# Inputs, lag chunks and weights in another order on one DMA queue, and the engines' work with them

## The chip, the cores and the metric

The kernel runs on one core of a Trainium2 chip. The metric is the device time of one execution in microseconds. An execution with the profiler on gives the trace; all times "at" a point are microseconds from the start of its span.

## The reference

```python
# x, ctx: (32, 128, 256) float32; w, u: (256,)
# 1. bidirectional RWKV mixing over the 128 tokens of a sequence, v = k = ctx, r = layernorm(x)
ek  = exp(k);  cur = exp(u + k)
wkv = (Af + Ab + cur * v) / (Bf + Bb + cur)      # Af[t] = sum over i<t of exp((t-1-i) w + k[i]) v[i], Ab the same from behind
x   = x + tanh(g_xattn) * sigmoid(r) * wkv       # Bf, Bb: the same sums without v
# 2. gated feed-forward in 8-bit steps, width 704
xq  = fake_quant(layernorm(x), clip_x)           # one scale over the whole tensor
h   = fake_quant(silu(xq @ Wgate.T) * (xq @ Wup.T), clip_down)
x   = x + tanh(g_ffn) * (h @ Wdown.T)            # weights quantised by row
```

## The kernel before

The program is written out engine by engine; each engine runs its own list in order and waits on semaphores. It has three stages, and the change lies in the first two.

**Stage 1, inputs (to about 33 us).** The 32 sequences are 8 groups of 4. SP loads x (`load_x`) and the context (`load_ctx`), one 512 KB transfer for a group, all on SP's queue. TensorE reverses each context group in time by a product with a flip matrix (`reverse`, L1043); ScalarE takes its exponential (`exp_k`, L538); VectorE multiplies that by the context (`product`, L742). The reversed groups share three pairs of PSUM banks, so `reverse(g)` waits for `product(g-3)`. For x, VectorE takes mean and variance (`stats1`, L760 and L764), GpSimd the reciprocal root (`rstd1`, L389 to L394) and ScalarE the exponential of the normalised x for the sigmoid (`exp_z`, L546). `idle_products` are products on TensorE whose results nobody reads.

**Stage 2, mixing (33 to 99 us).** The sums over tokens are products with a Toeplitz matrix for each of the 256 channels, 8 channels to a chunk, 32 chunks. ScalarE writes the 255 lag weights of each channel to DRAM once (`lag_weights`, stored with L534), and SP loads each chunk's matrices from there (`load_lags`, L309, 512 KB) into a ring of six slots that the context groups use first. Three chunks (`MADE`) are not loaded: ScalarE makes the exponentials (`make_lags`, L652, 8 instructions), and GpSimd prepares (`own_weights`, L419) and adds (`add_own`, L429) the diagonal. TensorE works the chunks in order (`accumulate(j)`, L1059, 16 matmul records each). The first waits for all eight `product`s; chunk j waits for its matrices and, from j = 6, for `mix(j-6)`, since six PSUM banks hold the sums. Chunks go on in pairs m: VectorE `denominator` (L799), ScalarE `reciprocal` (logarithm L554, exponential L557), VectorE `mix` (L811), GpSimd `residual` (L436). `denominator(0)` also waits for all eight `exp_z`. From pair 10 on, VectorE takes six early statistics for stage 3 in each pair (`early_stats`, L768).

Between the chunks the feed-forward weights are prepared: `load_weights` on SP, row maxima on VectorE (`weight_scales`, L750 to L752; for the third matrix also `down_diagonals`, L839), rounding and casting on ScalarE (`quantise_weights` L591, `cast_weights` L599), 12 transposes on TensorE (`turn_weights`, L1071) and a copy by ScalarE (`keep_weights`, L606, L609). A pair is finished by its last `mix`; the last one of all, `mix(31)`, opens stage 3.

**Stage 3, feed-forward (from 99 us)** begins with statistics of the mixed x. The change doesn't touch it.

A slot of the ring is asked for like this, on SP:

```python
before = GROUPS + j - SLOTS
if before < GROUPS:
    sp.wait_ge(s["ctx_back"], before + 1)
else:
    sp.wait_ge(s["ab_done"], before - GROUPS + 1)
```

Of the kernel before, what the change touches and what calls it, by code (L numbers as in the profile page):

```python
# [41 lines left out]
def gated_rwkv_ffn(nc, x, ctx_kv, g_xattn, g_ffn, w, u, clip_x, clip_down, w_gate, w_up, w_down, out):  # L42
# [4 lines left out]
    GROUPS = SEQS // GS  # L47
# [11 lines left out]
    CHUNKS = C // CK  # L59
# [2 lines left out]
    LAGS = 2 * T - 1  # L62
    SLOTS = 6

    MADE = 10, 14, 18

    BATCHES = [0], [1], [2, 3], [4, 5], [6, 7]
    BY_POOL = 1, 1, 1, 2, 2, 2, 2, 2
# [6 lines left out]
    with ExitStack() as stack:  # L75
# [40 lines left out]
        def loads_to(n):  # L116

            return len([i for i in range(n % SLOTS, n + 1, SLOTS) if i - GROUPS not in MADE])

# [165 lines left out]
        @block.sync  # L285
        def _(sp):
            def load_values(name, src):

                sp.dma_start(S[name], src.rearrange("(a b) -> a b", a=1).broadcast_to([P, 1])) \
                    .then_inc(s[name + "_in"], 16)  # L290

            def load_ctx(g):
                if g >= SLOTS:
                    sp.wait_ge(s["ctx_back"], g - SLOTS + 1)
                sp.dma_start(ring[g % SLOTS].rearrange("p (b c) -> p b c", c=C),
                             ctx_v[:, g * GS:(g + 1) * GS, :]).then_inc(ring_in[g % SLOTS], 16)

            def load_x(g):
                sp.dma_start(seqs(x_all, g * GS, GS), x_v[:, g * GS:(g + 1) * GS, :]).then_inc(x_in[g], 16)

            def load_lags(j):
# [6 lines that stand above are left out]
                src = bass.AP(lag_dram, j * CK * LAGS, [[1, P], [LAGS, CK], [1, T]])  # L308
                sp.dma_start(lag_tile(j), src).then_inc(ring_in[(GROUPS + j) % SLOTS], 16)  # L309

            def load_weights(m):

                if m < 2:
                    src = (w_gate, w_up)[m]
                    rows = w_nat[m].rearrange("p (k c) -> p k c", c=C)
                    sp.dma_start(rows[:, 0:KI, :],  # L316
                                 src[0:KI * P, :].rearrange("(k p) c -> p k c", p=P)).then_inc(weights_in[m], 16)
                    for half in range(2):
                        sp.dma_start(rows[half * IR:(half + 1) * IR, KI, :],
                                     src[KI * P:I, :]).then_inc(weights_in[m], 16)  # L320
                else:
                    down, src = w_nat[m].rearrange("p (h i) -> p h i", h=CH), w_down.rearrange("(h p) i -> p h i", p=P)
                    sp.wait_ge(s["w_quant"], 1)
                    sp.dma_start(down[:, :, 0:I], src).then_inc(weights_in[m], 16)
                    sp.dma_start(down[:, :, I:KA * P], src[:, :, KI * P:I]).then_inc(weights_in[m], 16)

            with nc.allow_non_contiguous_dma("256 values, once"):
                sp.dma_start(wu[:, 0:CG], w.rearrange("a b (p i) -> p (a b i)", i=CG)).then_inc(s["w_in"], 16)
                sp.dma_start(wu[:, CG:2 * CG], u.rearrange("a b (p i) -> p (a b i)", i=CG)).then_inc(s["u_in"], 16)
            load_values("g_x", g_xattn)  # L330
            for g in range(3):
                load_x(g)
            load_ctx(0)
            for g in range(3, 6):
                load_x(g)
                load_ctx(g - 2)
            load_ctx(4)
            load_ctx(5)
            load_x(6)
            load_ctx(6)  # L340
            load_ctx(7)
            load_x(7)
            sp.dma_start(w_all, w.rearrange("a b c -> (a b) c").broadcast_to([P, C])).then_inc(s["w_all_in"], 16)
            sp.dma_start(u_all, u.rearrange("a b c -> (a b) c").broadcast_to([P, C])).then_inc(s["u_all_in"], 16)
            sp.wait_ge(s["lag_stored"], 16)
            for j in range(CHUNKS):
                if j not in MADE:
                    load_lags(j)
                if j == 5:
                    load_weights(0)  # L350
                if j == 9:
                    load_weights(1)
                if j == 16:
                    load_weights(2)
                if j == 20:
                    load_values("g_f", g_ffn)
                    load_values("clx", clip_x)
                    load_values("cld", clip_down)

            for i, n in enumerate(pool_sums):  # L360
                sp.wait_ge(s["sum_done"], i + 1)
                sp.dma_start(out_v[:, 2 * n:2 * n + 2, :], seqs(x_all, 2 * n, 2)).then_inc(s["out_done"], 16)
            sp.wait_ge(s["out_done"], 16 * SUMS)
# [154 lines left out]
        def _(act):  # L518
# [17 lines left out]
            def exp_k(g):  # L536
                act.wait_ge(s["ctx_back"], g + 1)
                nc.scalar.activation(group(ek, g), turned(g).rearrange("p (b c) -> p c b", c=C), ACT.Exp).then_inc(s["ek_done"], 1)  # L538

            def exp_z(g):  # L540

                act.wait_ge(s["sc1_done"], g + 1)
                xs = seqs(x_all[:, :], g * GS, GS)
                for i in range(GS):
                    n = g * GS + i
                    last = nc.scalar.activation(ez[:, n, :], xs[:, i, :], ACT.Exp,  # L546
                                                scale=nr1[:, n:n + 1], bias=mr1[:, n:n + 1])
                last.then_inc(s["ez_done"], 1)
# [37 lines left out]
            def quantise_weights(m):  # L586

                act.wait_ge(s["w_rec"], m + 1)
                cols, parts, inverse = (C, KA, w_inv[:, m, :]) if m < 2 else (KA * P, CH, down_inv)
                for i in range(parts):  # L590
                    last = nc.scalar.activation(w_int[:, i * cols:(i + 1) * cols], w_nat[m][:, i * cols:(i + 1) * cols],  # L591
                                                ACT.Copy, scale=inverse[:, i:i + 1])
                last.then_inc(s["w_quant"], 1)
# [33 lines left out]

            lag_weights()
            for g in range(4):
                exp_z(g)  # L630
                exp_k(g)
            exp_k(4)
            exp_z(4)
            for g in range(5, GROUPS):
                exp_k(g)
            for g in range(5, GROUPS):
                exp_z(g)
            act.wait_ge(s["lag_abs_set"], 1)
            nc.scalar.activation(lag_abs, lag_abs, ACT.Abs).then_inc(s["lag_abs_set"], 1)
# [16 lines left out]
            for m in range(PAIRS - 1):  # L656
                reciprocal(m)
                if 2 * m + 6 in MADE:
                    make_lags(MADE.index(2 * m + 6))
                if m in (3, 7, 11):  # L660
                    quantise_weights((3, 7, 11).index(m))
                if m in (9, 13):
                    keep_weights((9, 13).index(m))
                if m in (5, 9, 13):
                    cast_weights((5, 9, 13).index(m))
                if m == 9:
                    exp_clips()
            for j in (CHUNKS - 2, CHUNKS - 1):
# [61 lines left out]
        def _(dve):  # L730
# [108 lines left out]
                    link(nc.vector.tensor_scalar(down_diag[:, h, :], ident[:, :], down_scale[:, h:h + 1], None,  # L839
                                                 ALU.mult))  # L840

            for g in range(4):
                stats1(g)
            product(0)
            stats1(4)
            product(1)
            stats1(5)
            for g in range(2, 5):
                product(g)
            stats1(6)  # L850
            for g in range(5, GROUPS):
                product(g)
            stats1(7)
            dve.wait_ge(s["lag_abs_set"], 2)
            nc.vector.tensor_scalar(lag_abs, lag_abs, -1.0, 0.0, ALU.add, ALU.max).then_inc(s["lag_abs_done"], 1)
# [3 lines left out]
            for m in range(PAIRS - 2):  # L859
                denominator(2 * m + 2)  # L860
                mix(2 * m)
                denominator(2 * m + 3)
                mix(2 * m + 1)
                if m == 2:
                    weight_scales(0)
                if m == 6:
                    weight_scales(1)
                if m == 9:
                    weight_scales(2)
                    dve.wait_ge(s["ident_set"], 2)  # L870
                    down_diagonals()
                    nc.vector.sem_inc(s["diag_done"], 1)
                if m == 10:
                    sigmoid_clips()
                if m > 9:
                    early_stats(done, 6)
                    done += 6
# [157 lines left out]
        def _(pe):  # L1035
# [58 lines left out]
            idle_products(12)  # L1094
            for g in range(GROUPS):
                reverse(g)
                if g < 4:
                    idle_products(5)
            for j in range(CHUNKS):
                accumulate(j)  # L1100
                if j in (14, 23):
                    turn_weights((14, 23).index(j))
            turn_weights(2)


# [121 lines left out]
```

## Time and profile before

| | us |
|---|---|
| median of 3 executions | 203.07 (202.43 to 203.27) |
| the profiled execution, its own time | 203.11 |
| its span, first to last instruction | 201.4 |
| TensorE busy / VectorE / ScalarE / GpSimd | 176.4 / 157.9 / 148.2 / 123.3 |
| bytes moved by DMA | 30.88 MB |

The profiled execution's own time is 1.7 us above its span, and 0.04 us above the median. Busy time is that of the whole span; on TensorE it contains the idle products.

### The profile page before, as it was taken

Reading aid. Unit: us, or ns where it says so; the run is one execution under the profiler, and the core shown is the slowest. Engines: PE = TensorE matmul, PEld = TensorE weight load, DVE = VectorE, ACT = ScalarE, POOL = GpSimd, SP = SyncE. Lnnn points to the kernel's source line nnn. Section 1 sums busy time; section 2 is a strip of 40 time slices with the busy share of each in tenths; the row PEclk is TensorE's granted clock in tenths of the full one; section 3 lists DMA queues with packets and bytes.
Section 4 is the critical chain, followed back from the end, with each engine's and each line's share of the span. In section 5 each row is a group of like instructions: output and inputs, shape, how many; then the busy total and the mean of one; then the engine's idle time right before and its main releaser. Section 6 shows DMA issues by size and latency. Waiting matters only on the chain.

```text
span 201.4 us, 3400 instructions
## 1 busy us (share of the span) xinstructions
PE 176.4 (88%) x1178; PEld 127.8 (63%) x1178; DVE 157.9 (78%) x355; ACT 148.2 (74%) x214; POOL 123.3 (61%) x142
## 2 busy tenths in 40 slices
PE   4589995997979999999959988999999996869990
PEld 4546643997979999999626753444343432658770
DVE  0669669263855777998999958599999998999992
ACT  3459889657498679559768989999798971999900
POOL 3365302565959935335689960989866772358892
PEclk9969999799999999999996999999999999999997
DMA  3999999999999999992000000000000000035555
GB/s 73 343 359 352 348 343 292 283 293 291 289 281 315 260 227 292 292 292 59 0 2 0 3 0 2 0 0 3 0 0 0 0 3 0 0 104 175 192 172 194
DMA packets 46448, 30.88 MB, mean 153 GB/s; under 512 B 2272, under 2 KB 46176, under 8 KB 46432
## 3 DMA queue, kind: packets, MB, share of 16 engines
q1 hardware_dynamic: 46016, 30.16, 53.0%
q10 hardware_dynamic: 416, 0.52, 0.7%
q8 instruction: 9, 0.15, 0.4%
q14 instruction: 7, 0.06, 0.1%
HBM read 26.22 MB, written 4.46 MB: 152 GB/s over the span
## 4 chain that ended last, share of the span: by engine, by line
PE 34%; DVE 25%; POOL 10%; DMA 10%; issue 6%; SPq 6%; ACT 5%; POOLq 1%; DVEq 0%; ACTq 0%
PE ps L1059 19%; PE ps L1043 8%; DMA hidden<-lag_w 6%; DVE h_peaks L952 6%; DVE z_t L1001 6%; PE ps L1162 4%; DVE hidden L941 4%; DMA hidden<-in_ctx 4%; POOL rs L406 3%; POOL hidden L475 2%; SPq L309 2%; PE ps L1090 2%; DVE z_t L1007 2%; DVE silu_out L1007 2%; SPq L316 2%
## 5 line engine op out<-in xcount | busy, mean ns | idle before, releaser
L1059 PE MATMUL ps<-hidden 128*128 128x128 f32 (+1 forms) x512 | 60.0, 280 | 4.8 <-DVE hidden L742 2.5
L1059 PEld LDWEIGHTS ps<-hidden 128*128 128x128 f32 x512 | 59.3, 196 | 6.0 <-issue 3.3
L436 POOL TENSOR_TENSOR x_all<-x_all,silu_out 128x512 f32<-128x512 f32 x15 | 23.0, 1537 | 19.4 <-DVE silu_out L811 19.4
L799 DVE SCALAR_TENSOR_TENSOR h_space<-z_t,ps 128x256 f32<-128x256 f32 x32 | 19.0, 598 | 12.2 <-PE ps L1059 11.9
L952 DVE TENSOR_REDUCE h_peaks<-hidden 128x1 f32<-128x1024 f32 (+1 forms) x24 | 26.0, 1124 | 0.2
L1198 PE MATMUL ps<-wdT,z_t 128*128 128x256 bf16 x192 | 22.4, 272 | 2.8 <-DVE z_t L1001 2.5
L1198 PEld LDWEIGHTS ps<-wdT,z_t 128*128 128x128 bf16 x192 | 17.8, 97 | 7.6 <-DVE z_t L1001 3.2
L702 ACT ACTIVATE silu_out<-ps,mix_scale 128x1024 f32<-128x1024 f32 (+1 forms) x18 | 18.4, 1020 | 2.1 <-PE ps L1162 2.0
L554 ACT ACTIVATE up_out<-h_space 128x512 f32<-128x512 f32 x15 | 9.4, 627 | 13.5 <-DVE h_space L799 13.5
L546 ACT ACTIVATE z_t<-x_all,mr,nr 128x256 f32<-128x256 f32 x32 | 16.4, 588 | 3.6 <-POOL mr L394 3.6
L1043 PE MATMUL ps<-hidden,flip 128*128 128x512 f32 x32 | 16.2, 647 | 3.2 <-DMA hidden<-in_ctx 3.2
L760 DVE BATCH_NORM_STATS2 bn<-x_all 128x6 f32<-128x256 f32 x32 | 11.2, 413 | 8.4 <-DMA x_all<-in_x 8.2
L811 DVE SCALAR_TENSOR_TENSOR silu_out<-ps,small,silu_out 128x256 f32<-128x256 f32 x32 | 15.2, 477 | 2.7 <-ACT silu_out L557 2.7
L722 ACT ACTIVATE h_space<-hidden,small 128x2560 int16<-128x2560 f32 (+1 forms) x9 | 17.1, 1942 | 0.3 <-DVE z_t L1001 0.3
L499 POOL TENSOR_TENSOR hidden<-h_space 128x1024 f32<-128x1024 f32 x6 | 14.7, 2447 | 3.9 <-ACT h_space L706 3.9
L514 POOL TENSOR_TENSOR x_all<-x_all,z_t 128x512 f32<-128x512 f32 x8 | 10.4, 1295 | 10.4 <-DVE z_t L1007 9.9
L499 POOL TENSOR_TENSOR hidden<-silu_out,up_out 128x1024 f32<-128x1024 f32 x6 | 14.2, 2361 | 3.8 <-ACT up_out L706 3.8
L941 DVE SCALAR_TENSOR_TENSOR hidden<-ps,mix_scale,silu_out 128x1024 f32<-128x1024 f32 (+1 forms) x12 | 13.2, 1101 | 2.9 <-ACT silu_out L702 2.8
L1118 PE MATMUL ps<-wgT,ident_b 128*128 128x512 bf16 x60 | 15.3, 396 | 0.0
L389 POOL TENSOR_TENSOR ve<-mv,consts 128x4 f32<-128x4 f32 x8 | 1.6, 199 | 20.4 <-DVE mv L764 20.4
L768 DVE BATCH_NORM_STATS2 bn<-x_all 128x6 f32<-128x128 f32 x64 | 13.5, 276 | 0.1
L1090 PEld LDWEIGHTS ps<-ident,flip 128*128 128x128 f32 x64 | 10.1, 240 | 5.0 <-POOL ident_b L378 2.8
(117 smaller groups left out, 340.3 us busy)
## 6 DMA issues: line engine op xcount, KB each, us to landing
hidden<-lag_w SPq DMA_DIRECT2D x29, 512.0 KB, 7.6
x_all<-in_x SPq DMA_DIRECT2D x8, 512.0 KB, 8.8
hidden<-in_ctx SPq DMA_DIRECT2D x8, 512.0 KB, 9.1
out<-x_all SPq DMA_DIRECT2D x15, 256.0 KB, 2.1
xq<-in_L_ffn_w_down SPq DMA_DIRECT2D x1, 704.0 KB, 5.8
xq<-in_L_ffn_w_gate SPq DMA_DIRECT2D x1, 640.0 KB, 7.3
h_space<-in_L_ffn_w_up SPq DMA_DIRECT2D x1, 640.0 KB, 6.0
out<-x_all ACTq DMA_DIRECT2D x1, 256.0 KB, 2.7
```

The costliest lines, as they stand in the source:

```text
L436: nc.gpsimd.tensor_tensor(xs, xs, mixed[:, m % 2, :, :].rearrange("p c b -> p b c"), ALU.add).then_inc(s["x1_done"], 1)
L499: nc.gpsimd.tensor_tensor(hidden[:, b * HB + k * BT:b * HB + (k + 1) * BT], silu_even[n % 2], up_even[n % 2], ALU.mult).then_inc(s["h_even ...
L546: last = nc.scalar.activation(ez[:, n, :], xs[:, i, :], ACT.Exp, scale=nr1[:, n:n + 1], bias=mr1[:, n:n + 1])
L702: nc.scalar.activation(silu_out[:, 1, 0:cols] if k % 2 else silu_even[even % 2], banks[0], ACT.Silu, scale=mix_scale[:, 0, k:k + 1]).then_ ...
L722: nc.scalar.activation(dst, inner(b, i, last, k, end), ACT.Copy, scale=S["inv_h"]).then_inc(s["h_int"], 1)
L799: nc.vector.scalar_tensor_tensor(den[:, m % 2, i * HALF:(i + 1) * HALF].rearrange("p (c b) -> p c b", b=SEQS), ez[:, :, j * CK:(j + 1) * C ...
L941: nc.vector.scalar_tensor_tensor(hidden[:, b * HB + k * BT:b * HB + k * BT + cols], ps[:, 6:8, :].rearrange("p a n -> p (a n)")[:, 0:cols] ...
L952: nc.vector.tensor_reduce(h_peaks[:, KA * b + k:KA * b + k + 1], hidden[:, b * HB + k * BT:b * HB + k * BT + cols], AX.X, ALU.max, apply_a ...
L1043: last = nc.tensor.matmul(turned(g)[:, half], flip[:, :], ring[g % SLOTS][:, half], start=True, stop=True)
L1059: last = nc.tensor.matmul(ps[:, j % BANKS, c * 2 * SEQS:end * 2 * SEQS], lag_tile(j)[:, c, :], ekp[:, (j * CK + c) * 2 * SEQS:(j * CK + en ...
L1118: nc.tensor.matmul(ps[:, bank, :], ident_b[:, :], wgT[:, 0, 0:512], start=True, stop=True)
L1198: last = nc.tensor.matmul(ps[:, n % 8, j * C:(j + 1) * C], hq[b % 2][:, at_:at_ + P], wdT[:, tile, :], start=(k == 0 and j == 0), stop=(k ...
```

## The change

It changes only the order of work; every instruction stays, and there are ten more idle products (20 stood between the reversals; now 16 stand between them and 14 behind them).

```diff
-    MADE = 10, 14, 18
+    MADE = 8, 12, 16
...
-            for g in range(3):
-                load_x(g)
+            load_x(0)
             load_ctx(0)
-            for g in range(3, 6):
-                load_x(g)
-                load_ctx(g - 2)
+            load_x(1)
+            load_ctx(1)
+            load_ctx(2)
+            load_x(2)
+            load_ctx(3)
             load_ctx(4)
+            load_x(3)
             load_ctx(5)
+            load_ctx(6)
+            load_x(4)
+            load_ctx(7)
+            load_x(5)
+            sp.wait_ge(s["lag_stored"], 16)
+            load_lags(0)
             load_x(6)
-            load_ctx(6)
-            load_ctx(7)
             load_x(7)
...
-            sp.wait_ge(s["lag_stored"], 16)
-            for j in range(CHUNKS):
+            for j in range(1, CHUNKS):
                 if j not in MADE:
                     load_lags(j)
-                if j == 5:
+                if j == 11:
                     load_weights(0)
-                if j == 9:
+                if j == 15:
                     load_weights(1)
-                if j == 16:
+                if j == 22:
                     load_weights(2)
...
             for g in range(4):
+                if g > 0:
+                    exp_k(2 * g - 1)
+                exp_k(2 * g)
                 exp_z(g)
-                exp_k(g)
-            exp_k(4)
-            exp_z(4)
-            for g in range(5, GROUPS):
-                exp_k(g)
-            for g in range(5, GROUPS):
+            exp_k(GROUPS - 1)
+            for g in range(4, GROUPS):
                 exp_z(g)
...
-                if m in (3, 7, 11):
-                    quantise_weights((3, 7, 11).index(m))
-                if m in (9, 13):
-                    keep_weights((9, 13).index(m))
-                if m in (5, 9, 13):
-                    cast_weights((5, 9, 13).index(m))
+                if m in (6, 8, 12):
+                    quantise_weights((6, 8, 12).index(m))
+                if m in (10, 13):
+                    keep_weights((10, 13).index(m))
+                if m in (7, 11, 14):
+                    cast_weights((7, 11, 14).index(m))
...
-            for g in range(4):
+            stats1(0)
+            stats1(1)
+            for g in range(3):
+                product(g)
+            stats1(2)
+            product(3)
+            product(4)
+            for g in range(3, 6):
                 stats1(g)
-            product(0)
-            stats1(4)
-            product(1)
-            stats1(5)
-            for g in range(2, 5):
-                product(g)
+                product(g + 2)
             stats1(6)
-            for g in range(5, GROUPS):
-                product(g)
             stats1(7)
...
-                if m == 2:
+                if m == 5:
                     weight_scales(0)
-                if m == 6:
+                if m == 7:
                     weight_scales(1)
-                if m == 9:
+                if m == 10:
                     weight_scales(2)
...
-                if g < 4:
-                    idle_products(5)
+                if g % 2 == 0:
+                    idle_products(4)
+            idle_products(14)
             for j in range(CHUNKS):
                 accumulate(j)
-                if j in (14, 23):
-                    turn_weights((14, 23).index(j))
+                if j in (20, 25):
+                    turn_weights((20, 25).index(j))
```

Where the change moves instructions: first SP's queue from the inputs to the weights (L309 is a chunk of lag matrices, L316 and L319 one of the first two weight matrices, L324 and L325 the third).

```order
-L299 DMA x_all<-in_x 128x4x256 x3
-L295 DMA hidden<-in_ctx_1024 128x4x256
...
-L343 DMA xq<-in_L0_xattn_w 128x256
-L344 DMA xq<-in_L0_xattn_u 128x256
-L309 DMA hidden<-lag_w 128x8x128 x6
+L309 DMA hidden<-lag_w 128x8x128
+L299 DMA x_all<-in_x 128x4x256 x2
+L349 DMA xq<-in_L0_xattn_w 128x256
+L350 DMA xq<-in_L0_xattn_u 128x256
+L309 DMA hidden<-lag_w 128x8x128 x10
```

One chunk now stands ahead of the last two groups of x, and ten (in place of six) ahead of the first weight matrix.

Then VectorE around the third weight matrix (L750/L754 row maxima, L839/L843 diagonals, L833/L837 and L834/L838 the clips, L768/L772 early statistics, L799/L803 and L811/L815 denominators and mixes). Before:

```order
L750 TENSOR_REDUCE small<-xq 128x2
L751 TENSOR_SCALAR small<-small 128x2
L752 RECIPROCAL small<-small 128x2
L839 TENSOR_SCALAR down_diag<-ident,small 128x128 x2
L799 SCALAR_TENSOR_TENSOR h_space<-z_t,ps 128x256
L811 SCALAR_TENSOR_TENSOR silu_out<-ps,small,silu_out 128x256
L799 SCALAR_TENSOR_TENSOR h_space<-z_t,ps 128x256
L811 SCALAR_TENSOR_TENSOR silu_out<-ps,small,silu_out 128x256
L833 TENSOR_SCALAR small<-small 128x1
```

And now:

```order
L803 SCALAR_TENSOR_TENSOR h_space<-z_t,ps 128x256
L815 SCALAR_TENSOR_TENSOR silu_out<-ps,small,silu_out 128x256
L754 TENSOR_REDUCE small<-xq 128x2
L755 TENSOR_SCALAR small<-small 128x2
L756 RECIPROCAL small<-small 128x2
L843 TENSOR_SCALAR down_diag<-ident,small 128x128 x2
L837 TENSOR_SCALAR small<-small 128x1
L838 RECIPROCAL small<-small 128x1
L837 TENSOR_SCALAR small<-small 128x1
L838 RECIPROCAL small<-small 128x1
L772 BN_STATS bn<-x_all 128x6 x6
```

The maxima and diagonals stood ahead of pair 10's denominators and mixes (chunks 22, 23) and now stand behind them, in one piece with clips and statistics.

Last, ScalarE at the end of stage 2 (L599/L604 the cast of the third matrix, L565/L570 and L568/L573 the half reciprocals of chunks 30 and 31). Before:

```order
L606 ACTIVATE wuT<-ps 128x1536
L599 ACTIVATE w_intb<-w_int 128x1536
L554 ACTIVATE up_out<-h_space 128x512
L557 ACTIVATE silu_out<-up_out 128x512
L565 ACTIVATE up_out<-h_space 128x256
L568 ACTIVATE silu_out<-up_out 128x256
```

And now:

```order
L611 ACTIVATE wuT<-ps 128x1536
L559 ACTIVATE up_out<-h_space 128x512
L562 ACTIVATE silu_out<-up_out 128x512
L604 ACTIVATE w_intb<-w_int 128x1536
L570 ACTIVATE up_out<-h_space 128x256
L573 ACTIVATE silu_out<-up_out 128x256
```

The cast stood ahead of the last whole reciprocal (pair 14) and now stands between it and the half reciprocal of chunk 30.

## Rows read from the trace of the kernel before

**Rows 1.** The page: granted TensorE clock in 40 slices; group of the reversals

```profile
PEclk9969999799999999999996999999999999999997
...
L1043 PE MATMUL ps<-hidden,flip 128*128 128x512 f32 x32 | 16.2, 647 | 3.2 <-DMA hidden<-in_ctx 3.2
```

**Rows 2.** Chain of waits, 80 to 125 us: start us, us, what

```profile
82.49 10.73 PE ps L1059 x96
...
98.83 0.45 DVE silu_out L811
```

**Rows 3.** Timeline, TensorE, 30 to 100 us: start us, us, engine, line, xcount [idle <-releaser]

```profile
33.47 12.53 PE L1059 MATMUL ps<-hidden 128*128 128x128 f32 x96 [2.46 <-DVE hidden L742]
47.16 9.14 PE L1059 MATMUL ps<-hidden 128*128 128x128 f32 x80 [1.16 <-DMA hidden<-lag_w]
57.45 7.38 PE L1059 MATMUL ps<-hidden 128*128 128x128 f32 x64 [1.14 <-DMA hidden<-lag_w]
...
65.33 16.49 PE L1059 MATMUL ps<-hidden 128*128 128x128 f32 x144
...
82.33 14.46 PE L1059 MATMUL ps<-hidden 128*128 128x128 f32 x128
```

**Rows 4.** Two windows: busy us of each engine, granted clock, DMA share, GB/s

```profile
15.00:30.00 15.00, 15.00 (x63) 8.78 (x62) 11.71 (x35) 13.30 (x23) 4.69 (x13) 1.00 1.10 349
30.60:69.06 38.46, 33.70 (x285) 32.92 (x284) 22.46 (x46) 28.24 (x63) 26.30 (x29) 0.96 1.10 292
```

**Rows 5.** DMA issue of u, the last before the chunks: KB, median us to landing

```profile
xq<-in_L_xattn_u SPq DMA_DIRECT2D x1, 128.0 KB, 6.5
```

**Rows 6.** Timeline, 0 to 45 us, and TensorE's weight loads at 69 us

```profile
13.87 1.41 DVE L760 BATCH_NORM_STATS2 bn<-x_all 128x6 f32<-128x256 f32 x4 [1.76 <-DMA x_all<-in_x]
14.56 1.02 ACT L538 ACTIVATE hidden<-ps 128x1024 f32<-128x1024 f32 x1 [2.37 <-PE ps L1043]
...
24.05 0.43 SPq L344 DMA_DIRECT2D xq<-in_L_xattn_u  x1
...
29.82 3.50 DVE L742 TENSOR_TENSOR hidden<-hidden,ps 128x1024 f32<-128x1024 f32 x3
...
34.67 0.38 DVE L764 BATCH_NORM_AGGREGATE mv<-bn 128x2 f32<-128x6 f32 x4
...
36.88 2.08 ACT L546 ACTIVATE z_t<-x_all,mr,nr 128x256 f32<-128x256 f32 x4 [0.89 <-POOL mr L394]
...
39.32 1.10 DVE L799 SCALAR_TENSOR_TENSOR h_space<-z_t,ps 128x256 f32<-128x256 f32 x2
...
40.54 0.63 ACT L554 ACTIVATE up_out<-h_space 128x512 f32<-128x512 f32 x1 [1.08 <-DVE h_space L799]
...
69.10 7.00 PEld L1059 LDWEIGHTS ps<-hidden 128*128 128x128 f32 x62 [0.17 <-DMA hidden<-lag_w]
```

**Rows 7.** Timeline, 45 to 60 us: the made chunk 10 on ScalarE and GpSimd

```profile
47.85 2.44 ACT L652 ACTIVATE hidden<-down_row,xq 128x128 f32<-128x128 f32 x8
49.20 1.28 POOL L429 TENSOR_TENSOR hidden<-hidden,up_out 128x512 f32<-128x512 f32 x1 [0.57 <-ACT hidden L652]
...
51.85 1.04 POOL L419 TENSOR_TENSOR up_out<-flip,xq 128x512 f32<-128x512 f32 x1
...
53.84 1.55 POOL L436 TENSOR_TENSOR x_all<-x_all,silu_out 128x512 f32<-128x512 f32 x1
```

**Rows 8.** Timeline, 79 to 99 us: VectorE's and ScalarE's end of stage 2

```profile
79.19 1.75 DVE L750 TENSOR_REDUCE small<-xq 128x2 f32<-128x1536 f32 x1
...
82.98 0.58 DVE L799 SCALAR_TENSOR_TENSOR h_space<-z_t,ps 128x256 f32<-128x256 f32 x1
...
85.81 0.58 DVE L799 SCALAR_TENSOR_TENSOR h_space<-z_t,ps 128x256 f32<-128x256 f32 x1
...
92.84 1.48 ACT L599 ACTIVATE w_intb<-w_int 128x1536 bf16<-128x1536 int8 x1
...
98.78 0.48 DVE L811 SCALAR_TENSOR_TENSOR silu_out<-ps,small,silu_out 128x256 f32<-128x256 f32 x1
```

## Prediction

> **What bounds the kernel now.** I read the chain of waits from its end first. From 82.5 us to 93.2 it is TensorE's chunk products, and from there to the last `mix` (it ends at 99.26) it is VectorE [rows 2, 8]. Behind that `mix` come stage 3's statistics and the feed-forward, which this change leaves alone. So the change is worth what it moves the end of `mix(31)`, and the rest of the text works that out.
>
> Next TensorE's timeline [rows 3]. A chunk takes 1.81 us (14.46 / 8, and 9.14 / 5 = 1.83). TensorE starts the chunks at 33.47, 2.46 us after its last reversal, released by the last `product`; it waits 1.16 and 1.14 us for loaded chunks 6 and 11, a last 0.17 at 69.1 for chunk 17 [rows 6], and from then on it is never idle: chunk 23 ends at 81.82 and chunk 31 at 96.8. Before 69 us stage 2 hangs on the queue, behind it on TensorE, at the very end on VectorE.
>
> The windows [rows 4] tell what the queue delivers: 349 GB/s while x and context come (1.50 us for 512 KB), 292 GB/s with chunks and weights (1.80 us a chunk, about TensorE's own pace). The reader is to see that two equal paces leave no room to catch up.
>
> **The inputs.** The fifth transfer landed at 13.87 [rows 6] (it was x group 3; it is context 2 now). From there, by durations: reversal 1.7 to 2.0 us (16.2 / 8, some at half clock [rows 1]), exponential 1.0 and `product` 1.2 (3.50 / 3) [rows 6], so `product(2)` ends near 17.9. Behind it VectorE's list has four `stats1` (1.41 + 0.38 + gaps, 1.9 each) and five `product`s, 13.6 us, and 0.6 of waiting for exponential 5, which stands behind `exp_z(2)`: `product(7)` ends at 32.1 and chunk 0 starts at 32.2, **1.3 us earlier**. TensorE's own list is no bound: context 7 is the thirteenth transfer, landing near 25.3, and with the 14 idle products TensorE is free near 30. That the eight context groups land 3 us earlier is thus half lost to VectorE.
>
> Two `stats1` now follow `product(7)`, not one. The last ends at 35.9, against 35.05 (34.67 + 0.38) [rows 6]; GpSimd's root and `exp_z(7)` follow as before, so `denominator(0)` starts at 40.2, **0.9 us later** than 39.32 [rows 6]. x 7 is in by 31.6, so its own lateness is hidden by VectorE. Chunks 0 to 5 need no `mix`, so this late start alone holds nobody up.
>
> **The made chunks.** Chunk 8's exponentials follow the second reciprocal. From `denominator(0)`: two denominators 1.1, reciprocal 1.3 (twice 0.63 [rows 6]), `mix` and `denominator(3)` 1.2, reciprocal 1.3, small gaps: 45.3. The whole piece on ScalarE and GpSimd took 3.9 us for chunk 10 (47.85 to 51.7, the second sum ending 1.28 + 1.27 behind 49.20 [rows 7]), so chunk 8 is ready at 49.2. TensorE, starting at 32.2, is through chunk 7 at 46.7, or near 47.5 with chunks 0 to 7 at the queue's pace: it waits some **2 us** at chunk 8. Even so chunk 8 starts earlier than before (47.16 + 2 x 1.81 = 50.8). From 8 to 16 GpSimd does, for every made chunk, two `own_weights` instructions, two `residual`s and two sums: 2.1 + 3.1 + 2.5 = 7.7 us [rows 7], where TensorE needs 7.3 for four chunks. Chunks 12 and 16 wait 0.4 us each: chunk 16 at 64.5. Then five chunks, one transposition (0.67, from 81.82 to 82.49 [rows 2, 3]) and two more: by TensorE and GpSimd chunk 23 could start at 78.0.
>
> **The queue.** Between u's landing (24.05 + 6.5 = 30.6 [rows 5, 6]) and chunk 17 (69.1) it delivered 16 chunks and three weight matrices, in 38.5 us. Now chunk 0 goes ahead, u lands near 32.4 (one chunk, 1.8, more in front), and up to chunk 23 come 20 chunks and again all three matrices: 38.5 + 4 x 1.81 = 45.7, so chunk 23 lands at 78.1, and the small values at chunk 20 make it 78.4. The weights are not taken off the path; they only move from ahead of chunk 17 to ahead of chunk 23. The queue and the made chunks give about the same time. I take 78.4 as start and 80.2 as **the end of chunk 23, 1.6 us earlier** than 81.82. Bounds: what a matrix costs the queue can be read three times. From 30.6 to 47.16 it brought 7 chunks and one matrix, 16.5 - 12.7 = 3.9 us; from there to 57.45 4 chunks and one, 3.0; to 69.1 5 chunks and one, 2.6 [rows 3, 6]. With all three at 2.6 chunk 23 lands at 76.7 (then GpSimd's 78.0 holds, and it ends at 79.8); with all at 3.9 at 80.6, and it ends at 82.4.
>
> The Trainium skill ("DMA: Bandwidth & Descriptors", Specifications) gives 512 B as the least transfer for line rate. The lag matrices' pieces are 512 B (128 float32), so by that rule chunks would land at x's pace, 1.50 us; the queue would then never bound chunk 23, and the sum would go by GpSimd's 79.8: 203.0. The trace disagrees: 292 against 349 GB/s [rows 4], and the measurement decides.
>
> **VectorE's end.** Behind the end of chunk 23 VectorE has, in order: `denominator(23)`, `mix(21)`, clips and statistics, as from 82.98 to 85.81, 2.8 us; now also the third matrix's maxima and diagonals, 79.19 to 82.98 less a denominator and a `mix`, 2.9 us; then everything from 85.81 to 99.26, 13.45 us, less about 0.5 that it waited in there for chunk 29 (the chain passes from TensorE to VectorE there [rows 2, 8]). That is 18.7. ScalarE adds to it: the cast (1.48 [rows 8]) now stands between the last whole reciprocal and the half one. Counted from `denominator(29)` the half reciprocal comes after 1.3 + 1.5 + 0.9 = 3.7 us, VectorE asks for it after 3.1: 0.6. Together `mix(31)` ends 19.3 us behind chunk 23, at **99.5**. Before it was 17.4. The maxima stood ahead of chunk 22's denominator then, in part while VectorE would have waited. TensorE's gain of 1.6 is spent on 2.9 of maxima and 0.6 of cast behind it, less the wait gone and less what VectorE had fallen behind.
>
> **Nothing or nearly.** The first two matrices' steps on VectorE and ScalarE sit where six banks give chunks a lead: `mix(11)` at 62 and chunk 17, which needs it, at 66. If that cover were gone each would cost what the third's does, some 2 us on VectorE. The transpositions are two between chunks before and after; the first now lies ahead of chunk 21, not 15, which changes no sum to chunk 23 (one before, one now: the second moved from behind 23 to behind 25). SP's wait for the stored lags is met: ScalarE issues the store ahead of its first exponential, and SP reaches the wait behind 14 transfers. Ten more idle products fill a wait.
>
> **Sum.** -1.6 (chunk 23) +1.9 (the way from there) = +0.3 us on the profiled 203.11, which is 0.04 above the median of the runs: **203.4**.
>
> **Rival A, faster.** TensorE's lead is kept. If the GpSimd pieces overlap better than chunk 10's row (chunk 8 ready by 48) and a matrix costs 2.6 us throughout, chunk 23 ends at 78.6, and `mix(31)` at 97.9: 1.4 us gained, 201.7. For it: the matrices cost less and less down the old queue, so the first one's 3.9 may be of its place. Against it: VectorE's 19.3 us are a row-by-row sum with no slack in it. Chance 0.24.
>
> **Rival B, slower.** The queue becomes the bound of the whole second half. Stage 2's transfers have 1.80 us a chunk against TensorE's 1.81; a matrix placed ahead of chunk 23 has no later stretch in which it is made good. Decisive is chunk 23's landing: each us beyond 78.4 goes through to the end. At 3.9 us a matrix it lands at 80.6, `mix(31)` ends at 101.7, 2.4 later: 205.5. For it: the waits at chunks 6 and 11 came right behind matrices [rows 3]. Against it: the third cost less than the first. A landing later than 79.2 turns the result to slower. Chance of that 0.20.
>
> **Rival C, the clock.** TensorE idles some 2 us ahead of chunk 0 and again ahead of chunk 8. Behind the idle 2.46 us ahead of the old chunk 0 the granted clock was at the 1.2 GHz level for a part of slice 8, which reads 7 [rows 1], and the first six chunks took 12.53 - 6 x 1.81 = 1.7 us too long [rows 3]. In the first place that is covered by the wait at chunk 8 (48.4 against 49.2). In the second it would cost up to 1.7 more: 205.1. It is part of B's chance.
>
> **Chances.** A measurement of this kernel tells about 0.5%, 1.0 us, from no change. Forecast, within that: 0.56; A 0.24; B with C 0.20. The range reaches down to A's price and up to 204.9, just short of C's; what is left out is B's far end and a little below A, under 2 in 10.
>
> **What would show it.** Chunk 0 near 32.2; `denominator(0)` near 40.2; an idle TensorE of about 2 us ahead of chunk 8, released by GpSimd's L434; the maxima L754 of the third matrix starting near 81.2; the last L815 ending near 99.5. Wrong if chunk 23 ends before 79 or after 81.5, or if VectorE needs other than 19 us behind it.

## The result and the profile after

The change makes the kernel slower, by about 1%. Both kernels were timed on the same chip, six runs each, and the change was timed a second time on another chip beside the first of the experiments on it:

| | before, us | the change, us | ratio, 95% interval |
|---|---|---|---|
| first comparison | 203.04 (201.47 to 203.27) | 204.52 (204.13 to 205.5) | 1.0094 [1.0056, 1.0131] |
| second | 202.73 | 204.28 | 1.0112 [1.0073, 1.0151] |
| profiled execution: own time, span | 203.11, 201.4 | 204.78, 203.0 | |
| end of chunk 23 | 81.82 | 81.91 | |
| end of the last `mix` | 99.26 | 100.90 | |
| last `mix` to the end of the span | 102.1 | 102.1 | |

The ratios here and below, but not the medians, leave out single executions more than 1.5% above the fastest of their kernel; there is one each in `e1_inputs_only`, `a1_scales9` and `a3_both`.

203.4 had been forecast, +0.3 us; it came out at +1.5. Behind the last `mix` the two kernels take the same 102.1 us (201.4 - 99.26, 203.0 - 100.90), so the whole loss lies ahead of the last `mix`, in the stages that the change touches, as the prediction had it.

The page of the kernel after: granted clock in 40 slices, and the groups of the reversals and of the chunk products.

```profile
PEclk9999999699999999999999999999999999999998
...
L1047 PE MATMUL ps<-hidden,flip 128*128 128x512 f32 x32 | 15.3, 611 | 1.8 <-DMA hidden<-in_ctx 1.7
...
L1063 PE MATMUL ps<-hidden 128*128 128x128 f32 (+1 forms) x512 | 59.8, 280 | 5.0 <-DMA hidden<-lag_w 3.9
```

Slice 8 of the clock reads 6 (7 before [rows 1]): in this execution too the granted clock fell to the 1.2 GHz level once in stage 2, here from 37.5 to 40.9 us, behind the wait for chunk 1. The reversals wait 1.8 us for context and not 3.2, and what the chunk products still wait for is mostly the queue: 3.9 of their 5.0 us.

TensorE's timeline of the kernel after, 30 to 101 us; a chunk is x16.

```profile
32.19 1.97 PE L1063 MATMUL ps<-hidden 128*128 128x128 f32 x16 [1.09 <-DVE hidden L746]
36.48 37.57 PE L1063 MATMUL ps<-hidden 128*128 128x128 f32 x320 [2.32 <-DMA hidden<-lag_w]
...
74.56 3.74 PE L1063 MATMUL ps<-hidden 128*128 128x128 f32 x32
79.90 5.63 PE L1063 MATMUL ps<-hidden 128*128 128x128 f32 x48 [1.61 <-DMA hidden<-lag_w]
...
86.04 10.88 PE L1063 MATMUL ps<-hidden 128*128 128x128 f32 x96
```

Chunk 0 runs alone, TensorE waits 2.32 us for chunk 1 to land, then twenty chunks follow without a gap (those of [rows 3] had waits at 6, 11 and 17). They take 37.57 us where 20 x 1.81 is 36.2; the difference is the slow stretch of the clock. It shows no cost at the end, since TensorE still waits 1.61 us for chunk 23 to land. That wait comes behind the load of the third matrix; chunk 23 starts at 79.90, as before (79.87). TensorE ends chunk 31 at 96.9, as before (96.8).

VectorE's timeline, 76 to 101 us: L803 is a denominator, L815 a `mix`, L754 the maxima of the third weight matrix.

```profile
78.84 0.47 DVE L815 SCALAR_TENSOR_TENSOR silu_out<-ps,small,silu_out 128x256 f32<-128x256 f32 x1
81.94 0.60 DVE L803 SCALAR_TENSOR_TENSOR h_space<-z_t,ps 128x256 f32<-128x256 f32 x1 [2.63 <-PE ps L1063]
82.45 0.48 DVE L815 SCALAR_TENSOR_TENSOR silu_out<-ps,small,silu_out 128x256 f32<-128x256 f32 x1
82.85 1.75 DVE L754 TENSOR_REDUCE small<-xq 128x2 f32<-128x1536 f32 x1
...
98.50 0.48 DVE L815 SCALAR_TENSOR_TENSOR silu_out<-ps,small,silu_out 128x256 f32<-128x256 f32 x1 [0.46 <-ACT silu_out L573]
...
100.42 0.48 DVE L815 SCALAR_TENSOR_TENSOR silu_out<-ps,small,silu_out 128x256 f32<-128x256 f32 x1
```

This is the view that tells the story. VectorE stands idle for 2.63 us until chunk 23 is through (79.90 + 2.01 = 81.91, the first `x16` of the chain below), and right behind that wait it does the maxima and diagonals, which in [rows 8] stood ahead of the same denominator, from 79.19. From 81.9 on VectorE is the bound.

The chain of waits of the kernel after, 59 to 99 us: start us, us, what.

```profile
59.93 11.50 PE ps L1063 x103
71.43 8.43 DMA hidden<-lag_w
79.90 2.01 PE ps L1063 x16
81.94 0.60 DVE h_space L803
...
82.93 1.67 DVE small L754
...
95.04 0.64 ACT up_out L559
...
96.24 0.14 ACT w_intb L604
...
97.61 0.41 ACT up_out L570
...
98.50 0.48 DVE silu_out L815
```

Before, the chain stayed with TensorE until 93.2 us and crossed to VectorE there [rows 2]. Now a landing hands it to TensorE for one chunk, and it crosses to VectorE at 81.94, at chunk 23. From there it passes through the maxima, and at 96.24 through the cast of the third matrix on ScalarE (L604), which the half reciprocal (L570) stands behind. Both had been priced.

### The profile page after: what moved, and what is told of

It is laid out like the page before. It is cut to its first block, busy times and chain, and to the rows that moved or that the text cites. A ratio compares the mean times of both kernels' runs of the same rounds, so it can differ in the third digit from the quotient of the medians.

```text
span 203.0 us, 3440 instructions
## 1 busy us (share of the span) xinstructions
PE 176.8 (87%) x1198; PEld 128.1 (63%) x1198; DVE 157.7 (78%) x355; ACT 148.6 (73%) x214; POOL 123.2 (61%) x142
## 4 chain that ended last, share of the span: by engine, by line
DVE 29%; PE 29%; DMA 13%; POOL 10%; issue 7%; ACT 6%; SPq 2%; POOLq 1%; DVEq 0%; ACTq 0%
PE ps L1063 18%; DMA hidden<-lag_w 8%; DVE h_peaks L956 6%; DVE z_t L1005 6%; PE ps L1047 5%; DMA hidden<-in_ctx 5%; PE ps L1167 4%; DVE hidden L945 4%; POOL rs L411 3%; DVE bn L772 2%; POOL hidden L480 2%; DVE z_t L1011 2%; DVE h_space L803 2%; DVE silu_out L815 2%; DVE silu_out L1011 2%
## 5 line engine op out<-in xcount | busy, mean ns | idle before, releaser
L803 DVE SCALAR_TENSOR_TENSOR h_space<-z_t,ps 128x256 f32<-128x256 f32 x32 | 19.1, 599 | 11.9 <-PE ps L1063 11.6
L815 DVE SCALAR_TENSOR_TENSOR silu_out<-ps,small,silu_out 128x256 f32<-128x256 f32 x32 | 15.2, 477 | 3.7 <-ACT silu_out L562 2.8
L1047 PE MATMUL ps<-hidden,flip 128*128 128x512 f32 x32 | 15.3, 611 | 1.8 <-DMA hidden<-in_ctx 1.7
L1094 PEld LDWEIGHTS ps<-ident,flip 128*128 128x128 f32 x84 | 12.1, 223 | 5.2 <-POOL ident_b L383 2.8
L1094 PE MATMUL ps<-ident,flip 128*128 128x128 f32 x84 | 12.3, 307 | 2.8 <-POOL flip L386 2.8
L1123 PE MATMUL ps<-wgT,ident_b 128*128 128x512 bf16 x60 | 14.4, 379 | 0.0
```

The source lines that it names most:

```text
L803: nc.vector.scalar_tensor_tensor(den[:, m % 2, i * HALF:(i + 1) * HALF].rearrange("p (c b) -> p c b", b=SEQS), ez[:, :, j * CK:(j + 1) * C ...
L815: nc.vector.scalar_tensor_tensor(mixed[:, m % 2, i * CK:(i + 1) * CK, :], half_bank(j, 1), S["tanh_x"], rden[:, m % 2, i * HALF:(i + 1) * ...
L1047: last = nc.tensor.matmul(turned(g)[:, half], flip[:, :], ring[g % SLOTS][:, half], start=True, stop=True)
L1094: nc.tensor.matmul(ps[:, TURN, 0:P], flip[:, :], ident[:, :], start=True, stop=True)
```

## The experiments

Two measures are used throughout: the median against the kernel before on the same chip, and, in the profiled execution, the way from the end of chunk 23 to the end of the last `mix` (17.4 us before, 19.0 in the change). The end of a chunk is the end of its sixteenth product. Five executions with the change's queue ended chunk 23 anywhere between 80.4 and 82.1 us, so a verdict rests on medians, and on the way behind chunk 23, which repeats to 0.2 us where VectorE's list is the same.

### One part of the change at a time

`e1_inputs_only`: the new order of inputs, exponentials, products and early statistics, all else as before. It was timed twice, the second time as `e1b_inputs_only`; the trace of the first has a span of 457.9 us and tells nothing, so the rows are the second's.

```diff
-    MADE = 8, 12, 16
+    MADE = 10, 14, 18
...
-                if j == 11:
+                if j == 5:
                     load_weights(0)
```

(and so on for every weight step, back to its place in the kernel before).

> Only the order of the inputs (SP, ScalarE, VectorE, idle products, chunk 0 ahead of x 6 and 7); made chunks and weights as before. Two parts theory (the loss is the third matrix ahead of chunk 23 plus its maxima and cast behind it): no loss worth the name here, 202.5 to 203.5 us, TensorE starts chunk 0 near 32.2, and the last mix ends within 0.5 us of 99.3. Rival, the inputs (the queue loses 2 us around chunk 0 and x 6, as u landed at 34.65 and not 32.4): the whole 1.5 us are here, 204.5 us, last mix near 100.9, chunk 17 landing 70.5 or later.

> The order of the inputs alone once more, since the profile of the first run is unusable: 203.3 us, 0.3 per cent above before. In the profile chunk 0 starts near 32.2 and denominator(0) 0.7 to 1.0 us later than 39.3; the queue is through with chunk 17 no earlier than 69.1.

Measured: 203.34, ratio 1.0034 [1.0016, 1.0051], and again 203.09, 1.0012 [0.9992, 1.0032]. The 1.5 us are not here, and the earlier start buys nothing. TensorE's timeline of the second:

```profile
32.08 1.97 PE L1063 MATMUL ps<-hidden 128*128 128x128 f32 x16 [0.93 <-DVE hidden L746]
35.96 9.16 PE L1063 MATMUL ps<-hidden 128*128 128x128 f32 x80 [1.91 <-DMA hidden<-lag_w]
47.32 18.07 PE L1063 MATMUL ps<-hidden 128*128 128x128 f32 x144 [2.20 <-DMA hidden<-lag_w]
```

What chunk 0 gains is waited out at chunk 1 (1.91) and at chunk 6 (2.20), both times for the queue.

`e2_made_only`: the kernel before with chunks 8, 12 and 16 made on chip.

```diff
-    MADE = 10, 14, 18
+    MADE = 8, 12, 16
```

> Only chunks 8, 12, 16 made in place of 10, 14, 18. Two parts theory: 203.0 plus or minus 0.5; chunk 8 is ready near 48.3, ahead of its turn at 50.8, and the number of loaded chunks ahead of chunk 19 is the same. Rival, GpSimd (7.7 us of work for four chunks that TensorE does in 7.3): a wait for chunks 12 and 16, up to 1 us lost, 204.

Measured: 203.3, 1.0038 [1.0016, 1.0059]. TensorE waits 2.07 us at chunk 6, for a landing, and the chunk 8 behind it costs no wait; GpSimd, the rival, holds nobody up, and the small loss has no cause shown.

`e3_weights_only`: the kernel before with all weight steps moved as in the change, the queue's loads included.

```diff
-                if j == 5:
+                if j == 11:
                     load_weights(0)
...
-                if m in (5, 9, 13):
+                if m in (7, 11, 14):
-                    cast_weights((5, 9, 13).index(m))
+                    cast_weights((7, 11, 14).index(m))
...
-                if m == 9:
+                if m == 10:
                     weight_scales(2)
```

> Only the weights' places (loads behind chunks 11, 15, 22, and their maxima, rounding, casts, copies, transpositions); inputs and made chunks as before. Two parts theory: TensorE is ahead in the middle, then waits at chunk 23 for the queue, which lands near 78 to 79.5; the last mix comes 19.2 us behind chunk 23's end (17.4 before), so 99 to 100.5: 203.0 to 204.3 us. Rival, the inputs: no loss here, 202.5 to 203.0.

Measured: 202.88, 1.0011 [0.9986, 1.0035], no difference. Its profile shows both sides that the prediction weighed: chunk 23 ends at 80.3, 1.5 us earlier than in the kernel before, and the way from there is 19.0 us, 1.6 longer, as in the change; the last `mix` ends at 99.27, where it did. With the old inputs the forecast exchange takes place.

`e4_inputs_made`: the change with the weight steps where they were before.

> The whole change without the weights' part. Two parts theory: all that cost time is out: 202.3 to 203.3 us, last mix 17.5 us behind chunk 23's end. Rival, the inputs: 204.5 us, as the change itself.

Measured: 203.45, 1.0053 [1.0026, 1.008], just above the 202.3 to 203.3 that were expected, though the way behind chunk 23 is 17.4 us, as in the kernel before. Its profiled execution was its fastest (202.6), with the last `mix` ending at 98.65, so the profile alone would have told a gain where the median tells a loss.

The parts give 1.0012 to 1.0034, 1.0038 and 1.0011: together 0.6 to 0.8%, against 0.9 to 1.1 for the whole. They do not add cleanly (see the next four runs), but nothing in them is a gain.

### Where in the change the loss sits

These four were timed on one chip. `a0_change` is the change once more.

> The change itself again, as the measure for the three beside it: 204.5 us, 0.7 to 0.9 per cent above the kernel before. Its last mix 19.2 us behind the end of chunk 23.

Measured: 204.28, 1.0112 [1.0073, 1.0151]. Its timeline of TensorE:

```profile
35.26 12.83 PE L1063 MATMUL ps<-hidden 128*128 128x128 f32 x112 [1.14 <-DMA hidden<-lag_w]
48.64 7.36 PE L1063 MATMUL ps<-hidden 128*128 128x128 f32 x64 [0.55 <-POOL hidden L434]
56.27 7.36 PE L1063 MATMUL ps<-hidden 128*128 128x128 f32 x64 [0.28 <-POOL hidden L434]
63.89 9.14 PE L1063 MATMUL ps<-hidden 128*128 128x128 f32 x80 [0.26 <-POOL hidden L434]
...
78.86 5.63 PE L1063 MATMUL ps<-hidden 128*128 128x128 f32 x48 [1.58 <-DMA hidden<-lag_w]
```

With chunk 1 landed earlier (35.26), the made chunks come out as forecast in kind: waits for GpSimd's L434 at chunks 8, 12 and 16. Chunk 23 ends at 80.87 and the last `mix` at 99.84: 19.0 us again. The clock did not fall in stage 2 of this execution, and the loss is the same.

`a1_scales9`: the third matrix's maxima and diagonals back ahead of chunks 22 and 23. The load stays behind chunk 22.

```diff
-                if m == 10:
+                if m == 9:
                     weight_scales(2)
```

> The change with the third matrix's maxima and diagonals back behind mix 19 (pair 9) in place of behind mix 21 (pair 10). Two parts theory: in the change VectorE stands idle 2.6 us there while chunk 23's matrices are late, and does the 2.9 us of maxima after it; put back they fill the wait, the last mix comes 1.5 us earlier and the time is 203.0 us. Rival, the queue alone: VectorE's place doesn't matter, TensorE's late chunks set the end: 204.5 us.

Measured: 202.82, 1.0008 [0.9986, 1.0029]. **One step moved back takes the loss away**: 1.46 us of 1.55. VectorE's timeline:

```profile
77.47 1.75 DVE L754 TENSOR_REDUCE small<-xq 128x2 f32<-128x1536 f32 x1
...
80.34 0.60 DVE L803 SCALAR_TENSOR_TENSOR h_space<-z_t,ps 128x256 f32<-128x256 f32 x1 [0.21 <-DVE down_diag L843]
80.86 0.48 DVE L815 SCALAR_TENSOR_TENSOR silu_out<-ps,small,silu_out 128x256 f32<-128x256 f32 x1
81.81 0.60 DVE L803 SCALAR_TENSOR_TENSOR h_space<-z_t,ps 128x256 f32<-128x256 f32 x1 [0.48 <-PE ps L1063]
...
99.25 0.48 DVE L815 SCALAR_TENSOR_TENSOR silu_out<-ps,small,silu_out 128x256 f32<-128x256 f32 x1
```

The maxima now run in part while TensorE waits for chunk 23 (1.46 us, until 79.78). That puts chunk 22's denominator late (80.34), and VectorE is still at chunk 23's on time (it even waits 0.48). Chunk 23 ends at 81.8, as in the change's first profile, but the last `mix` ends 18.0 us behind it, at 99.73, and not 19.0.

`a2_cast13`: only the cast of the third matrix moved back ahead of the last whole reciprocal.

```diff
-                if m in (7, 11, 14):
-                    cast_weights((7, 11, 14).index(m))
+                if m in (7, 11, 13):
+                    cast_weights((7, 11, 13).index(m))
```

> The change with the third matrix's cast back behind pair 13 in place of pair 14. Two parts theory: VectorE waits 0.46 us for ScalarE ahead of mix 30, TensorE 0.84 ahead of its last transposition; 0.5 us less, 204.0 us. Rival, the queue alone: no difference, 204.5 us.

Measured: 204.06, 1.0068 [1.0041, 1.0095]; the way behind chunk 23 is 18.8. The interval overlaps that of `a0_change`: the cast alone is worth 0.2 us or nothing that these runs can tell.

`a3_both`: both edits together.

> Both, maxima and diagonals behind pair 9 and the cast behind pair 13. Two parts theory: the way from chunk 23's end to the last mix is 17.4 us as before, or what chunk 31's end (96.9) allows, 2.4 us behind that: last mix near 99.3, 203.0 us or a little less. Rival, the queue alone: 204.5 us.

Measured: 202.6, 0.9997 [0.997, 1.0023]. In its profile chunk 23 was even later than in the change:

```profile
80.14 5.61 PE L1063 MATMUL ps<-hidden 128*128 128x128 f32 x48 [2.81 <-DMA hidden<-lag_w]
```

and the last `mix` ends at 99.62, 17.5 us behind that chunk:

```profile
76.91 1.75 DVE L754 TENSOR_REDUCE small<-xq 128x2 f32<-128x1536 f32 x1 [0.34 <-DMA xq<-in_L_ffn_w_down]
...
99.14 0.48 DVE L815 SCALAR_TENSOR_TENSOR silu_out<-ps,small,silu_out 128x256 f32<-128x256 f32 x1
```

Chunk 23 started 0.2 us later than in the change's first profile (80.14 against 79.90), and the median is 1.7 us lower (202.6 against 204.28): a late chunk 23 alone is not what separates the change from this version.

### The same step moved in the kernel before

`b1_before_late_max`: nothing in the queue, the inputs or the made chunks is touched.

```diff
-                if m in (5, 9, 13):
-                    cast_weights((5, 9, 13).index(m))
+                if m in (5, 9, 14):
+                    cast_weights((5, 9, 14).index(m))
...
-                if m == 9:
+                if m == 10:
                     weight_scales(2)
```

> The kernel before, inputs, made chunks and loads untouched, with the third matrix's maxima and diagonals moved from pair 9 to pair 10 and its cast from pair 13 to pair 14. Two parts theory: this alone takes the way from chunk 23's end to the last mix from 17.4 to 19.2 us, and costs 1.5 to 1.8 us: 204.4. Rival, the queue or the inputs: nothing in the queue is moved, so 202.8.

Measured: 204.03, 1.0065 [1.0041, 1.0088], +1.4 us on its chip's 202.61 (1.5 to 1.8 had been expected). VectorE's timeline:

```profile
81.82 1.74 DVE L750 TENSOR_REDUCE small<-xq 128x2 f32<-128x1536 f32 x1
...
97.43 0.48 DVE L811 SCALAR_TENSOR_TENSOR silu_out<-ps,small,silu_out 128x256 f32<-128x256 f32 x1 [0.47 <-ACT silu_out L568]
...
99.35 0.48 DVE L811 SCALAR_TENSOR_TENSOR silu_out<-ps,small,silu_out 128x256 f32<-128x256 f32 x1
```

Chunk 23 ends at 80.64 and the last `mix` at 99.83: 19.2 us, where the change has 19.0. Two steps that add no work and displace no transfer cost what the change costs, nearly. Maxima and cast were moved together here; each alone was not tried in this kernel.

`w1_weights_early_max`: `e3` with the maxima at m == 9 and the cast at 13.

> The kernel before with the weights' part of the change, but the third maxima at pair 9 and its cast at pair 13 as before; inputs and made chunks as before. With the weights' part alone chunk 31 ended near 95.5, 1.3 us earlier than before, and the last mix at 99.3; with the maxima put back the last mix follows chunk 31 by 2.5 to 3 us, 98.0 to 98.5: 201.6 to 202.2 us, faster than both kernels. Rival, the queue: 202.9.

Measured: 202.3, 0.9995 [0.9971, 1.002]. Chunk 23 ends at 79.4, 2.4 us earlier than in the kernel before, and the last `mix` at 98.77. 201.6 to 202.2 had been expected; the median equals the kernel before, so most of those 2.4 us are lost again, and TensorE's timeline says where:

```profile
73.86 5.52 PE L1059 MATMUL ps<-hidden 128*128 128x128 f32 x48
80.04 3.81 PE L1059 MATMUL ps<-hidden 128*128 128x128 f32 x32 [0.66 <-DMA hidden<-lag_w]
84.73 0.84 PE L1071 MATMUL ps<-ident_b,w_intb 128*128 128x128 bf16 x12 [0.88 <-ACT w_intb L599]
85.41 10.88 PE L1059 MATMUL ps<-hidden 128*128 128x128 f32 x96
```

TensorE waits 0.66 us for chunk 24 to land and 0.88 for the second matrix's cast ahead of its transposition behind chunk 25; chunk 31 ends at 96.3, 0.5 earlier than before. In this kernel, the kernel before and `a3_both` alike the last `mix` ends 2.5 us behind chunk 31: once VectorE's list is short enough, TensorE's last chunks are the bound again.

`w2_third_load_20`: `w1` with the third matrix loaded two chunks earlier, to give the maxima room.

```diff
-                if j == 22:
+                if j == 20:
                     load_weights(2)
```

> The same with the third matrix loaded behind chunk 20 in place of 22, so that its maxima never wait for it. If the lateness at chunk 23 matters, the wait only moves to chunk 21: the same as the run beside it within 0.3 us, 201.6 to 202.2.

Measured: 203.42, 1.0028 [1.0008, 1.0049], 1.1 us slower than `w1`, where the same time had been expected. TensorE's timeline:

```profile
63.94 9.33 PE L1059 MATMUL ps<-hidden 128*128 128x128 f32 x80 [0.60 <-DMA hidden<-lag_w]
...
74.94 5.64 PE L1059 MATMUL ps<-hidden 128*128 128x128 f32 x48 [0.99 <-DMA hidden<-lag_w]
...
81.90 3.79 PE L1059 MATMUL ps<-hidden 128*128 128x128 f32 x32 [1.31 <-DMA hidden<-lag_w]
```

The chunks lag behind TensorE from chunk 21 on, and the last `mix` ends at 99.54, 0.8 us later than in `w1`.

None of these versions beats the kernel before: `w1` and `a3_both` equal it.

## Why the prediction was wrong

No change was forecast (+0.3 us, chance 0.56), and a loss was measured, which had 0.20. The measured 204.52 lies inside the range. The step that failed is the credit for chunk 23: its end was to come 1.6 us earlier and did not; the charge set against it was right. Step by step:

- **Chunk 0 at 32.2**: 32.19. **`product(7)` to 32.1**: 32.04. **`denominator(0)` at 40.2**: 40.40. **Chunk 8 ready at 49.2**: 49.40. The row-by-row sums held.
- **TensorE idle 2 us ahead of chunk 8**: wrong in its place. The first profile has 2.32 us at chunk 1 instead, for the queue; the second (`a0_change`) 1.14 there and 0.55 ahead of chunk 8. The waits of 0.4 at chunks 12 and 16 measured 0.28 and 0.26 in the second.
- **u lands near 32.4**: 34.65, and in the four other executions with the change's queue (`a0` to `a3`) 33.45 to 34.66. This is where the credit was lost. From u to chunk 23 the queue took 45.2 us (34.65 to 79.86) where 45.7 and 0.3 had been reckoned, and 44.7 to 45.6 in the others: the price of chunks and matrices was right, its starting point was not. With the old inputs and the same places of the weights u landed at 30.9 and 31.2, and chunk 23 did end early, at 80.3 (`e3`) and 79.4 (`w1`).
- **The end of chunk 23, 1.6 us earlier (80.2)**: 81.91, 0.1 later; 80.87 in the second profile. The failed step. The five executions give 80.4 to 82.1, 81.4 on average; with the old order of inputs and weights it was 81.82 and, in `b1`, 80.64. The medians agree: 1.6 us lost behind chunk 23 and 1.5 in all leave no gain that can be told. One of the prediction's own signs of being wrong, an end after 81.5, was met. A second fault was the footing: a credit of 1.6 us was claimed on the 81.82 of one execution, a time that varies by 1.2 with the same queue. The drop of the clock [rows 1] was not what made it late: chunk 5 ended at 46.00 with the drop and at 46.11 in `b1` without one, but chunk 6 could start at 47.16 and 46.54, chunk 11 at 57.45 and 56.37, when their matrices landed.
- **19.3 us from chunk 23 to the last `mix`, 17.4 before**: 19.0 in both profiles of the change and in `e3`, 19.2 in `b1`. This term was right, and it is the loss. By the rows: 2.80 us of maxima and diagonals and the new wait of 0.46 for ScalarE, less the 1.13 by which VectorE had been late at chunk 23's denominator before (1.16 us behind the chunk, now 0.03) and its old wait of 0.53 for chunk 29, make 1.6.
- **The rivals.** B had named a landing beyond 79.2 as what makes the change slower. The first profile has 79.86; but the second landed at 78.81 and its median is as slow, and with the maxima moved back `a1` and `a3` recover the time with landings at 79.74 and 80.10. The queue is only the missing credit. Rival A's claim that the matrices grow cheap fell with the queue's 45.2 us. Of rival C's two drops of the clock one came, in the first profile, behind chunk 1's wait; it was covered by the wait at chunk 23, and the second profile has the loss without it.
- **The end of the kernel unmoved**: 102.1 us on both sides.

The Trainium skill ("DMA: Bandwidth & Descriptors", Specifications) would have chunks of 512 B pieces land at x's pace; this was weighed before and the trace preferred. The measured 45.2 us for 20 chunks and three matrices again speak for the trace: at 1.50 us a chunk they would have taken 6 less.

What stays open: why u landed late, for which the last section has a likely but unproven part; and the parts' own small losses. The inputs cost 0.1 to 0.3% and the made chunks 0.4% alone, and yet with `a1`'s edit the three parts together cost nothing measurable. With the weights at their old places, TensorE waits for landings at chunk 6 in both (2.20, 2.07); that the weights' move lifts just this is likely, but was only argued.

## What to carry to other kernels

Find the last long wait of the engine that ends a stage, and ask of each step whether it stands ahead of that wait or behind. Ahead, it can be free; behind, it can cost up to its length, here 1.4 us of 203 for 2.8 us of VectorE's work and a cast that were only moved. And set a certain cost against a doubtful credit as what they are: VectorE's list behind chunk 23 took 19.0 to 19.2 us in four executions, while the landing that opens chunk 23 came anywhere between 78.3 and 80.1 in five.

## What the runs showed of the hardware

**Some landings are late when a packet of the instruction queue runs.** In stage 2 the trace has a packet of 16 KB on the queue called `instruction` every 14 to 17 us (30.1, 47.2, 61.8, 77.4 us in the change). The window of DMA at 30 us in the change:

```profile
q1 hardware_dynamic: 166, 0.17, 105.1%
q8 instruction: 1, 0.02, 14.4%
```

and x 6, in flight then, issued at 21.8:

```profile
L299 SPq DMA_DIRECT2D x_all<-in_x x1: 2877/2877/2877, 21.8 to 21.8; - x1
...
DMA to landing us min/median/max: 10.6/10.6/10.6
```

It landed at 32.32, 3.06 us behind chunk 0 (29.26), where the pace is 1.50. The same transfer in `e4_inputs_made`, whose program is the same up to there:

```profile
L299 SPq DMA_DIRECT2D x_all<-in_x x1: 2876/2876/2876, 21.6 to 21.6; - x1
...
DMA to landing us min/median/max: 9.0/9.0/9.0
```

It landed at 30.55, though such a packet ran at 29.5. In the change chunk 23 came 3.06 us behind the matrix ahead of it (79.86 against 76.80) with a packet at 77.4, and in the kernel before chunk 3 came 3.43 us behind chunk 2 (39.41) with one at 37.1; that lateness is part of the 3.9 us which the prediction read as the first matrix's price. In the thirteen traces that can be read, 17 transfers of x or lag matrices between 24 and 92 us landed over 2.8 us behind the one ahead. In 10 of these cases a packet of this queue had started in between, in the other 7 less than 1 us before the earlier landing; but 48 of the 65 packets of that stretch went by without such a lateness. x 6 accounts for some 1.5 of the 2.3 us by which u was late in the change; in `e4`, where none of these transfers came late, u landed at 33.07 and not at the 32.4 of the prediction, so the rest has another cause. The link is inferred from the times, and no run took the packets away.

**The clock did not fall every time.** TensorE idled 2.46 us ahead of chunk 0 in the kernel before, and six chunks took 12.53 us, partly at the 1.2 GHz level [rows 1, 3]. The same 2.46 us idle ahead of the same chunks stood in five more executions: in `w1` the granted clock fell too (0.50 from 35.2 to 38.6 us), in `e2`, `e3`, `b1` and `w2` it did not, and in `e2` and `b1` the six chunks took 10.90, TensorE's full pace. In the change it fell behind 2.32 us idle at chunk 1, and in `a3` it did not behind 2.55. So whether it falls behind a gap of this length changed from one execution to the next. The row of `b1_before_late_max`:

```profile
35.21 10.90 PE L1059 MATMUL ps<-hidden 128*128 128x128 f32 x96 [2.46 <-DVE hidden L742]
```
